# Feed-forward tiles on one Trainium2 core: three subtractions moved ahead of one product on VectorE

## The reference, cut to what matters

```
def fp4_linear(x, w):
    xq = fp4_quant_dequant(x)       # blocks of 16: scale = max|x| / 6, round to the FP4 grid, scale back
    wq = fp4_quant_dequant(w)
    return einsum('bsk,nk->bsn', xq, wq)
gate = fp4_linear(x, w_gate)        # 512 -> 1408
y    = fp4_linear(x, w_up)          # 512 -> 1408
h    = silu(gate) * y
out  = fp4_linear(h, w_down)        # 1408 -> 512; h is quantised too
```

## Time and profile before

| | |
|---|---|
| median of 3 runs | 5159.74 us (5157.7 to 5160.44) |
| the profiled execution | 5163.48 us |
| its span, first to last instruction | 5161.3 us |
| busy: TensorE, VectorE, ScalarE, GpSimd | 92%, 93%, 65%, 74% |
| mean granted TensorE clock, as a share of full speed | 0.975 |
| from the stored tiles to near the end (3640 to 5090 us) | 59 tiles and a part, TensorE busy 1441.92 of 1450 us, VectorE 1232.28 |

### The profile page before, as it was taken

The page is one execution under the profiler, slowest core; times in us unless marked ns, Lnnn a source line. Parts: engine busy times, 40 slices in busy tenths (PEclk is TensorE's granted clock), DMA queues, the critical chain, the costliest instruction groups (busy, mean ns, idle before and its releaser), DMA issues. The chain is left out here.

```text
span 5161.3 us, 67236 instructions
## 1 busy us (share of the span) xinstructions
PE 4767.4 (92%) x21964; PEld 3287.6 (64%) x21964; DVE 4794.1 (93%) x5476; ACT 3336.1 (65%) x7037; POOL 3831.4 (74%) x1722
## 2 busy tenths in 40 slices
PE   8799899998999999989899999968999999999999
PEld 3555555555555555555555555555888888888888
DVE  8999999999999999999999999997888888888887
ACT  3777877777777777787777877765444444444442
POOL 6999999999999999999999999994223222322221
PEclk9899999999999999999999999978999999999999
DMA  7555565555656656556556665553000110011000
GB/s 258 180 194 194 190 203 187 195 194 192 201 188 198 195 189 197 191 192 200 189 193 192 197 200 187 188 172 138 31 31 31 33 35 31 31 34 34 31 31 29
DMA packets 402675, 745.79 MB, mean 144 GB/s; under 512 B 44083, under 2 KB 44211, under 8 KB 402198
## 3 DMA queue, kind: packets, MB, share of 16 engines
q1 hardware_dynamic: 401590, 738.08, 43.8%
q0 software_dynamic: 736, 3.41, 0.2%
HBM read 698.05 MB, written 43.26 MB: 144 GB/s over the span
## 5 line engine op out<-in xcount | busy, mean ns | idle before, releaser
L712 POOL TENSOR_TENSOR slot<-du,b_row 128x1024 f32<-128x1024 f32 x1024 | 2394.5, 2371 | 2.9 <-DMA b_row<-b_c_rows 2.9
L1045 DVE TENSOR_TENSOR_SCAN decays<-decays,state,slot 128x512 f32<-128x512 f32 x1376 | 1687.1, 1271 | 61.2 <-POOL slot L712 54.8
L912 ACT ACTIVATE decays<-delta,rate 128x512 f32<-128x512 f32 x2048 | 1385.1, 687 | 49.1 <-DVE slot L993 0.7
L1106 PE MATMUL work_ps<-h_t,win 128*128 128x512 f32 x2048 | 978.4, 625 | 138.5 <-ACT delta L848 109.8
L1183 PEld LDWEIGHTS y_ps<-ident,slot 128*128 128x128 f32 x8192 | 946.5, 143 | 237.3 <-issue 177.8
L1183 PE MATMUL y_ps<-ident,slot 128*128 128x128 f32 x8192 | 1021.3, 277 | 41.7 <-POOL slot L719 29.1
L1568 POOL TENSOR_TENSOR hq<-hid,qinv 128x1408 f32<-128x1408 f32 x63 | 163.4, 2594 | 1018.5 <-DVE qinv L1594 1018.5
L1052 DVE TENSOR_TENSOR slot<-decays,c_row 128x512 f32<-128x512 f32 x1376 | 871.4, 674 | 3.3 <-DMA c_row<-b_c_rows 3.3
L719 POOL TENSOR_TENSOR slot<-slot,c_row 128x1024 f32<-128x1024 f32 x336 | 795.2, 2367 | 82.3 <-ACT state L901 80.2
L1045 DVE TENSOR_TENSOR_SCAN slot<-decays,state,slot 128x512 f32<-128x512 f32 x672 | 819.2, 1263 | 4.2 <-POOL slot L712 2.2
L1106 PEld LDWEIGHTS work_ps<-h_t,win 128*128 128x128 f32 x2048 | 392.7, 200 | 589.3 <-issue 491.8
(11 more groups left out here) (274 smaller groups left out, 7359.3 us busy)
## 6 DMA issues: line engine op xcount, KB each, us to landing
b_row<-b_c_rows SPq DMA_DIRECT2D x1024, 256.0 KB, 3.9
c_row<-b_c_rows SPq DMA_DIRECT2D x1024, 256.0 KB, 3.8
win<-in_w_in SPq DMA_DIRECT2D x256, 256.0 KB, 4.4
xt<-in_x SPq DMA_DIRECT2D x16, 1024.0 KB, 6.7
xr<-in_x SPq DMA_DIRECT2D x64, 256.0 KB, 4.3
x_after_mamba<-xr SPq DMA_DIRECT2D x64, 256.0 KB, 4.6
xa<-x_after_mamba SPq DMA_DIRECT2D x64, 256.0 KB, 3.0
xres<-x_after_mamba SPq DMA_DIRECT2D x64, 256.0 KB, 2.7
```

Source lines behind the costliest of these rows:

```text
L712: pool.tensor_tensor(slot[:, u % SLOTS, :, :], du[:, p % 2, :, :], two(b_row[:, u % BC_RING, :]), ALU.mult).then_inc(S["ub_ready"], 1)
L912: act.activation(decay[u % 2][:, i, :], delta[:, p % 2, i, :], ACT.Exp, scale=rate[:, 2 * p + i, n:n + 1]).then_inc(S["decay_ready"], 1)
L1045: dve.tensor_tensor_scan(d if u in DVE_C else h, d, h, state[:, 2 * p + i, n:n + 1], ALU.mult, ALU.add).then_inc(S["scan_done"], 1)
L1106: op = pe.matmul(dst[:, :], win[:, i % WIN_RING, k, :], h_t[:, k, :], start=(k == 0), stop=(k == KT - 1))
```

## The change

In the body of every tile but the first, VectorE's `product(t, 1)` is moved from ahead of the three low parts of tile t-1 to behind them. No instruction is added or taken away on any engine, and no semaphore or count changes. The order on VectorE becomes: quantise_x(t+1), three low parts of t-1, product(t,1), product(t,2), x_low(t+1).

```diff
                         if exists_tile(ahead) and not opens(ahead) and not opens(t):
                             quantise_x(ahead)
-                        if exists_tile(t) and not opens(t):
-                            product(t, 1)
                         if closes(before):
                             end_lo(1)
                             end_lo(2)
                         elif exists_tile(before):
                             for i, (k, n) in enumerate(TURNS):
                                 wait(dve, S["h_hi"], before.at(3, i + 1))
                                 dve.tensor_tensor(hh[1][:, k:k + n, :], turn_ps[i][:, 0:n, :], hh[0][:, k:k + n, :].bitcast(F32),
                                                   ALU.subtract).then_inc(S["h_lo"], 1)
+                        if exists_tile(t) and not opens(t):
+                            product(t, 1)
                         if exists_tile(t) and not opens(t):
                             if closes(t):
                                 end_quantise(1)
```

## The result

| | before | after |
|---|---|---|
| median | 5159.74 us | 5185.47 us (5184.55 to 5188.52, 5 runs) |
| ratio | | 1.0052, 95% interval 1.004 to 1.0064 |
| profiled execution, its span | 5163.48, 5161.3 us | 5184.55, 5182.4 us |
| mean period of a tile | 24.553 us | 25.013 us |
| mean granted clock | 0.975 | 0.977 |

The change costs 25.7 us, 0.5%. The forecast was 5184.7.

The account below looks back on a forecast made before the run. VectorE's gapless chain was taken as the bound, its period growing from 24.553 real to 24.98 us; 60 tiles gave 25.6 us, less 0.6, so 5159.74 + 25.0 = 5184.7 us, range 5177 to 5195.

Parts of the forecast that it names:

- The bound: VectorE's in-order chain has no hole except its 2.7 us wait for GpSimd's division, though VectorE is only 85% busy.
- The chain of 24.27: VectorE's time in us from one x_low to the next, in a tile where it waits for nobody but GpSimd.
- The stall: Ahead of product(t,2), VectorE stands still 0.7 us because nothing covers the third group's Silu any more.
- the period of 25.13: Upper bound per tile, if ScalarE doesn't overlap the Silu with x_high; the time would be 5193.8 us.
- The period: VectorE's new x_low to x_low: 21.54 + 1.66 + 1.78 = 24.98 us, against 24.553 real before.
- The sum: 60 periods from tile 1 to 61 add 25.6 us, less 0.6 for the earlier `down` in tile 61: 25.0 us.
- its own period: TensorE's time from one tile's first gate product to the next one's when it doesn't wait: 24.34 us.
- the friction in before: TensorE and VectorE delay each other in turns, 0.21 us per tile above TensorE's own 24.34.
- the first rival: The earlier low parts release `down` and the Silu costs VectorE nothing: period 24.34, 12.8 us faster, 5147.0 us; chance 0.03.
- What hides the rest: Layer norm on ScalarE and GpSimd keeps its 0.65 us distance to VectorE's rounding addition, which stays 2.59 us.
- The second, half hidden: Rival of no change: the stall is partly hidden, period 24.38 to 24.72 us, time within 10 us of before; chance 0.05.
- The third: Rival, slower still: layer norm shifts against the rounding (5221 us) or the clock drops to 0.94 (5240 us); chance 0.05.

Follow-up runs that it names:

- with slack on VectorE too: The changed order with two act_gate buffers and x_low moved into VectorE's wait for GpSimd's division, against before: 5140.05 us, ratio 0.9946 to 0.9973.
- the order of before with x_low in the gap: Before, with x_low moved from the tile's end into VectorE's wait for GpSimd's division (behind hidden_scales, ahead of hidden_round): 5139.0 us, ratio 0.9946 to 0.9971.
- x_low in the gap and the changed order: After, with x_low moved from the tile's end into VectorE's wait for GpSimd's division: 5157.92 us, ratio to before 0.9986 to 1.0004.

## Why the prediction was right

**The bound.** Right. VectorE's gapless chain was the thing to read, not its 85%. The chain of 24.27 came back as 24.26 with two act_gate buffers.

**The stall.** Right in place and size. Forecast from the start Q of the moved product: Silu at Q + 0.78, product(t,2) at Q + 1.30, x_low at Q + 1.78. Measured: 0.77 (4411.98 to 4412.75), 1.29 (4413.27), 1.78 (4413.76). The bracket says 0.62 us and not 0.7, because the product lasts 0.68 and the next independent instruction could have started 0.60 behind its start; by starts, VectorE loses 1.29 - 0.60 = 0.69. ScalarE did overlap the Silu with x_high (0.39 from start to start), so the period of 25.13 didn't come.

**The period.** 24.98 forecast. From the first low part of tile 1 (3610.05) to that of tile 61 (5110.85) there are 1500.8 us, 25.013 per tile. Single tiles have 24.99 to 25.00. Two tiles are longer, 25.34 and 25.62 (4213.44 to 4238.78 and 4988.70 to 5014.32), which is 0.96 us in all. VectorE's wait ahead of L1668 (`add_down`) in both is 0.57 us where it is 0.21 elsewhere, and in the second the stall is 0.90 us and not 0.62. Before has the same 0.57 us in two tiles (4223.48 and 4984.69), so that wait is not made by the change. What makes it was not tried.

**The sum.** The tiles gave 60 x (25.013 - 24.553) = 27.6, less 0.6 at the end, 27.0 where 25.0 was forecast; the two traces give 27.2 from the first changed instruction to the end. The profiled execution grew by only 21.07 us, since its first affected tile began 6.14 us earlier (3610.05 against 3616.19), in a part of the program that the change doesn't touch. The medians differ by 25.7. The period was forecast 0.03 us too short, which is 2 us in 60 tiles, and the part ahead of the tiles differed by several us between the two traces; that the median came within 0.8 us of 5184.7 is therefore partly luck.

**TensorE.** One term was mis-sized: its own period is 24.22 and not 24.34 us, so the friction in before is 0.33 and not 0.21 us. The forecast survived because TensorE isn't the bound of the changed kernel: only its waiting is longer (25.00 - 24.22 = 0.78 us where I had 0.64), and it lies where it was forecast, ahead of turn_x (0.28) and of `down` (0.99 us behind turn_x and not 0.50). It would have mattered in the first rival, which I priced at 5147: two act_gate buffers, the same case made real, gave 5144.6, and with slack on VectorE too 5140.

**What hides the rest.** Right. The rounding additions last 2.60 and 2.59 us as before, the clock stays at 1.00, and the layer norm keeps its distance: GpSimd's scale starts 7.97 us behind x_high (4413.14 to 4421.11), and VectorE's addition 0.66 us behind the scale (forecast 0.65).

**The rivals.** The first came true only with the edit that takes its obstacle away. The second, half hidden, is what the kernel with the product behind the second low part is: there VectorE's chain is 24.54 us, inside the 24.38 to 24.72 of that rival, and nothing shows. The third didn't occur.

## What to carry to other kernels

An engine at 85% busy can be the bound when its in-order queue has a wait that nothing can fill: follow one period of it and count the holes, and compare the length with the other engine's own period, taken from a stretch without waits. Before an instruction is moved, look at what it releases on another engine and who needs that next: work that stands between a release and its use is cover, and taking it away lengthens the engine's chain by what the round trip exceeds the cover by. The time grows only by what is left once the chain has used up the room that it had. Here, with no cover left, the chain grew by 0.73 us (24.27 to 25.00) and the room was 0.28 us (24.55 - 24.27), so about 0.45 us per tile showed; with 0.47 us of cover the chain grew to 24.54 and nothing showed. If the new order is wanted for another reason, give the round trip a second buffer first.

## What the runs showed that was not expected

**A wait without a mark.** A distance of 0.65 us between two weight loads where the free one is 0.50, with no idle time in brackets. A period "without waits" should be checked against a kernel or a tile in which the suspected releaser is clearly early.

**GpSimd and VectorE hold each other up in turns.** In the order of before with x_low in the gap, GpSimd's layer norm falls differently against the rounding (GpSimd first, then VectorE):

```profile
4422.62 2.40 POOL L1573 TENSOR_TENSOR hn<-hn,scale_row 128x512 f32<-128x512 f32 x1 [2.26 <-ACT hn L1489]
4425.10 2.55 POOL L1575 TENSOR_TENSOR hn<-hn,shift_row 128x512 f32<-128x512 f32 x1
```

```profile
4422.24 1.63 DVE L1602 TENSOR_TENSOR hq<-hq,hstep 128x1408 f32<-128x1408 f32 x1
4423.90 2.60 DVE L1604 TENSOR_TENSOR hq<-hq,hstep 128x1408 f32<-128x1408 f32 x1
4426.53 2.60 DVE L1606 TENSOR_TENSOR hq<-hq,qscale 128x1408 f32<-128x1408 f32 x1
```

VectorE's addition started 0.38 us before GpSimd's scale and lasts 1.63 us; the scale lasts 2.40. With x_low in the gap and the changed order it is the other way:

```profile
4408.50 1.29 POOL L1573 TENSOR_TENSOR hn<-hn,scale_row 128x512 f32<-128x512 f32 x1 [1.75 <-ACT hn L1489]
```

```profile
4408.64 2.64 DVE L1602 TENSOR_TENSOR hq<-hq,hstep 128x1408 f32<-128x1408 f32 x1
```

GpSimd started 0.14 us earlier and lasts 1.29 us, and the addition 2.64. In these rows the one that starts first is not slowed. The Trainium skill, SBUF — State Buffer, section SBUF: two separate sides, says that a VectorE instruction with two SBUF inputs and a GpSimd one that reads SBUF take a shared pair of ports as an exclusive lock: the first to start has it for its whole length, and the other waits. An estimate by that rule is 4423.87 - 4422.62 + 1.29 = 2.54 us for the scale, where the row has 2.40, and 4409.79 - 4408.64 + 1.62 = 2.77 for the addition, where the row has 2.64: it agrees within 0.14 us.

The scale of before lasts 1.76 us and not 1.29, though it starts ahead of the addition (4412.13). It starts while another VectorE instruction runs:

```profile
4411.85 0.90 DVE L201 TENSOR_SCALAR hstep<-hstep 128x1408 f32<-128x1408 f32 x1
```

So which instruction of VectorE the scale meets has to be read over the whole chain, and not for the addition alone. That this row makes the scale longer was not tried. In both orders of the kernels with x_low in the gap two of VectorE's instructions lose about 1 us each; a shift of half a microsecond moved the loss from the first and second to the second and third and didn't lower it.
